# Attention loops of a four-layer GNN: SyncE awaits the ring's place before it loads row numbers, and a gather waits for the row numbers only

## The chip, the cores and the metric

The kernel runs on 1 core of one Trainium2 chip. Its time is the device time of one execution in microseconds (us). Before the change it is 5852.53 us, the median of 3 runs (5847.59 to 5857.74).

## The reference

Four graph layers follow each other on x (3125 nodes x 256 features, 100000 edges sorted by their target node), each behind a layer norm and a ReLU, each added to x. What matters here are layers 1 and 2, which hold the three attention loops:

```python
def _gatv2(x, src, dst, eattr, Wl, Wr, We, att, b, n):      # layer 1, twice
    xl = x @ Wl; xr = x @ Wr; ee = eattr @ We
    xj = xl[src]
    h = leaky_relu(xj + xr[dst] + ee, 0.2)
    logits = h @ att
    ex = exp(logits - segment_max(logits, dst, n)[dst])
    alpha = ex / segment_sum(ex, dst, n)[dst]
    return segment_sum(xj * alpha[:, None], dst, n) + b

# layer 2: four heads of 64
h = (x @ W).reshape(-1, 4, 64)
e = leaky_relu(einsum(h, att_src)[src] + einsum(h, att_dst)[dst], 0.2)
alpha = softmax of e over the edges of one dst
out = sigmoid(segment_sum(alpha[:, :, None] * h[src], dst).reshape(-1, 256) + bias)
```

Layer 0 is a weighted sum over neighbours, layer 3 a graph convolution; both are done by dense matrices of node pairs and are not touched.

## The kernel before

The edges are cut into 220 groups (NG) of 512 edges (4 tiles, T, of 128), all of a group with targets in one block of 128 nodes. A node stage writes a table of one row of 264 floats per node to DRAM. Then an attention loop goes over the groups: `edges1` and `edges2` (`gatv2_loop`, layer 1, once for each of its two convolutions), and `gat_edges` (`gat_loop`, layer 2).

The five engines run their own written-out programs and meet through semaphores. Each engine works in steps; in step s it handles group s minus the lag of the piece at hand, so that several groups are in flight. In `gatv2_loop`:

- GpSimd (POOL) gathers: for group t four indirect DMAs (L909), one per tile, take 128 table rows each by the row numbers in `m.src_col[t % 10]` and put them in the place `m.gath[t % 10]` of a ring of RG = 10 places (five are the buffer called gath, five lie in h, so a trace shows both names).
- SyncE (SP) loads: `load_list` brings the row numbers of group t from `g_src` into `src_col` (L889, 2 KB); `load` brings lin (L894, 2 KB), locrow (L895, one row laid out over 128 partitions, 128 KB) and eaT (L896, 12 KB) into rings of R = 5 places. SP is a queue in order: an instruction that waits holds all loads behind it.
- ScalarE (ACT) turns locrow into a 0/1 matrix of who is whose target (`place`, L1007 and L1010, lag 0), and copies and exponentials.
- TensorE (PE): `mix` (L1049, L1052, lag 1), `show_logits` (lag 3), `flip` (lag 4) and `sum_group` (L1071, lag 4), the last reader of the gathered rows, which raises `group_sum`.
- VectorE (DVE): `sum_inputs` (L921, lag 2) is the first reader of the gathered rows and waits for them; then `dot` (L928), `see` (L934), `add_linear` (L939, which raises `logits`), `add_group` (L980, lag 5), and small casts.

In `gat_loop` the same loads and gathers are L1111, L1117 and L1129. DVE does `place` (L1144, lag 0), reads the gathered rows first at L1157 (lag 1), weighs them at L1202 (lag 3), and does many pieces of 16 or 4 columns, some of them casts to bf16 (L1170, L1178, L1224, L1240); PE's last reader is `sum_group` (L1367, lag 4).

Before the change the place of group t in the ring of gathered rows is awaited by POOL: its first gather waits for `listed` (the row numbers have landed) and for `group_sum` of group t-10 (the place is free). In between it raises a semaphore `begun` that nobody waits for. SP loads the row numbers of group t once `logits` of group t-10 is there, and the three inputs of group t-5 directly behind it, on the same condition.

Of the kernel before, what the change touches and what calls it, by code (L numbers as in the profile page):

```python
# [32 lines left out]
R = 5  # L33
RG = 10
# [51 lines left out]
def drow(t, g):  # L86

    return t[bass.ds(g, 1), :].rearrange("a n -> (a n)")
# [28 lines left out]
def straight(stages, blocks=None, total=NG, unroll=U):  # L117

    deepest = max(lag for lag, _ in stages)
    of = [None] * total  # L120
    for s in range(total + deepest):
        if blocks and s % unroll == 0 and s < total:
            of[s:s + unroll] = blocks(s, unroll, s // unroll)
        for lag, stage in stages:
            t = s - lag
            if 0 <= t < total:
                stage(t, t % unroll, t // unroll, of[t])
# [12 lines left out]
def after(eng, sem, t, back=0, each=1):  # L140

    if not isinstance(t, int) or t >= back:
        eng.wait_ge(sem, (t - back + 1) * each)


def nth(u, turn, ring, unroll=U):

    return turn * (unroll // ring) + (u // ring + 1)
# [710 lines left out]
def gatv2_loop(nc, m, name, table, c):  # L859
# [6 lines left out]
    K = 3 * T  # L866
    with stage_of(nc, name) as (st, block):
        arrived, listed = st.sems("arrived", R), st.sems("listed", RG)
        gathered, begun = st.sems("gathered", RG), st.sem("begun")
        distance = st.sem("distance")  # L870
        placed, masked, mixed, summed = (st.sem(k) for k in ("placed", "masked", "mixed", "summed"))
        dotted, logits, hi_made, rest_made = (st.sem(k) for k in ("dotted", "logits", "hi_made", "rest_made"))
# [3 lines left out]
        weights, group_sum, done = (st.sem(k) for k in ("weights", "group_sum", "done"))  # L876
# [5 lines left out]
        @block.sync  # L882
        def _(sp):
            def by_column(src, t):
                return drow(src, t).rearrange("(p j) -> p j", j=T)

            def load_list(t, u, turn, b):
                after(sp, logits, t, RG)
                sp.dma_start(m.src_col[u % RG][:, :], by_column(m.g_src, t)).then_inc(listed[u % RG], 16)  # L889

            def load(t, u, turn, b):
                r = u % R
                after(sp, logits, t, R)
                sp.dma_start(m.lin[r][:, :], by_column(m.g_lin[c], t)).then_inc(arrived[r], 16)  # L894
                sp.dma_start(m.locrow[r][:, :], drow(m.g_locb, t).partition_broadcast(P)).then_inc(arrived[r], 16)  # L895
                sp.dma_start(m.eaT[r][0:KE, :], m.g_eaT[bass.ds(t, 1), :, :].rearrange("a k n -> (a k) n")  # L896
                             ).then_inc(arrived[r], 16)

            straight([(0, load_list), (RG - R, load)])

        @block.gpsimd
        def _(pool):
            def gather(t, u, turn, b):
                r = u % RG
                pool.wait_ge(listed[r], 16 * nth(u, turn, RG))
                after(pool, group_sum, t, RG)
                pool.sem_inc(begun, 1)
                for j in range(T):
                    pool.indirect_dma_start(m.gath[r][:, j, :], None, table,  # L909
                                            bass.IndirectOffsetOnAxis(m.src_col[r][:, j:j + 1], 0)  # L910
                                            ).then_inc(gathered[r], 16)

            straight([(0, gather)])
# [165 lines left out]
def gat_loop(nc, m, name, table):  # L1079
# [7 lines left out]
    WA = H * (DH + 1)  # L1087
    with stage_of(nc, name) as (st, block):
        arrived, listed = st.sems("arrived", R), st.sems("listed", RG)
        gathered, begun = st.sems("gathered", RG), st.sem("begun")  # L1090
        placed, masked, mixed, summed = (st.sem(k) for k in ("placed", "masked", "mixed", "summed"))
        pairs, logits, hi_made, rest_made = (st.sem(k) for k in ("pairs", "logits", "hi_made", "rest_made"))
        mid_made, parts, turned, copied = (st.sem(k) for k in ("mid_made", "parts", "turned", "copied"))
# [5 lines left out]
        group_sum, rescaled, done = (st.sem(k) for k in ("group_sum", "rescaled", "done"))  # L1099
# [7 lines left out]
        @block.sync  # L1107
        def _(sp):
            def load_list(t, u, turn, b):
                after(sp, logits, t, RG)  # L1110
                sp.dma_start(m.src_col[u % RG][:, :], drow(m.g_src, t).rearrange("(p j) -> p j", j=T)  # L1111
                             ).then_inc(listed[u % RG], 16)

            def load(t, u, turn, b):
                r = u % R
                after(sp, logits, t, R)
                sp.dma_start(m.locrow[r][:, :], drow(m.g_locb, t).partition_broadcast(P)).then_inc(arrived[r], 16)  # L1117

            straight([(0, load_list), (RG - R, load)])

        @block.gpsimd
        def _(pool):
            def gather(t, u, turn, b):
                r = u % RG
                pool.wait_ge(listed[r], 16 * nth(u, turn, RG))
                after(pool, group_sum, t, RG)
                pool.sem_inc(begun, 1)
                for j in range(T):
                    pool.indirect_dma_start(m.gath[r][:, j, :], None, table,  # L1129
                                            bass.IndirectOffsetOnAxis(m.src_col[r][:, j:j + 1], 0)  # L1130
                                            ).then_inc(gathered[r], 16)

            straight([(0, gather)])
# [669 lines left out]
def build(nc, a, out):  # L1803
    m = Memory()
    with ExitStack() as ctx:
# [82 lines left out]
        for c in (1, 2):  # L1888
            gatv2_nodes(nc, m, a, f"gatv2_{c}", c, tables[c - 1])
            gatv2_loop(nc, m, f"edges{c}", tables[c - 1], c)  # L1890
            batch_norm(nc, m, f"bn{c}", c, residual=(c == 2))
        layer_norm(nc, m, "ln2")
        gat_nodes(nc, m, a, "gat", tables[2])
        gat_loop(nc, m, "gat_edges", tables[2])
        gat_out(nc, m, "gat_out")
        layer_norm(nc, m, "ln3", scale=m.dinv)
# [37 lines left out]
```

## Time and profile before

| | |
|---|---|
| median of 3 runs | 5852.53 us |
| profiled execution, its own time | 5865.7 us |
| span of that execution in the trace | 5863.4 us |
| mean granted TensorE clock | 0.954 of full speed |
| PE busy | 4774.3 us, 81% |
| DVE busy | 4688.4 us, 80% |
| POOL busy | 3357.2 us, 57% |
| ACT busy | 3334.6 us, 57% |

Busy shares are means over the whole program; stages differ. The three attention loops take about 1131, 1131 and 1250 us of the span. A row of a timeline names the start, the duration, the engine, the line, and the tiles written and read; in brackets stands how long the engine sat idle before, and what ended it. "issue" means that the engine waited for nothing that the trace shows. Rows of SPq are the times at which SyncE issues a DMA, not the transfer. Ends of matmuls are modelled.

### The profile page before, as it was taken

Reading aid. Unit: us, or ns where it says so; the run is one execution under the profiler, and the core shown is the slowest. Engines: PE = TensorE matmul, PEld = TensorE weight load, DVE = VectorE, ACT = ScalarE, POOL = GpSimd, SP = SyncE. Lnnn points to the kernel's source line nnn. Section 1 sums busy time; section 2 is a strip of 40 time slices with the busy share of each in tenths; the row PEclk is TensorE's granted clock in tenths of the full one; section 3 lists DMA queues with packets and bytes.
Section 4 is the critical chain, followed back from the end, with each engine's and each line's share of the span. In section 5 each row is a group of like instructions: output and inputs, shape, how many; then the busy total and the mean of one; then the engine's idle time right before and its main releaser. Section 6 shows DMA issues by size and latency. Waiting matters only on the chain. (4 is left out here: it accounts for less than half of the span.)

```text
span 5863.4 us, 117927 instructions
## 1 busy us (share of the span) xinstructions
PE 4774.3 (81%) x30318; PEld 3499.0 (60%) x30319; DVE 4688.4 (80%) x18137; ACT 3334.6 (57%) x8375; POOL 3357.2 (57%) x3590
## 2 busy tenths in 40 slices
PE   0699888789779999998589999998377777777599
PEld 0344544568567777776277777776255555555388
DVE  4899999830588889888789888888699999999701
ACT  0677676610366667665466666666366666666500
POOL 1344444346477777776477777776177777777100
PEclk9899999889899999999899999999699999999899
DMA  4112233368255555554055555553154444444253
GB/s 91 33 57 81 88 97 100 100 234 308 100 128 135 134 134 135 134 135 107 31 138 134 134 134 135 134 134 90 48 131 123 120 120 119 120 120 121 68 148 110
DMA packets 591145, 695.30 MB, mean 119 GB/s; under 512 B 227684, under 2 KB 497297, under 8 KB 584443
## 3 DMA queue, kind: packets, MB, share of 16 engines
q0 software_dynamic: 128832, 362.75, 24.3%
q1 hardware_dynamic: 462010, 329.68, 20.7%
q14 instruction: 256, 2.09, 0.1%
q8 instruction: 47, 0.77, 0.1%
HBM read 589.91 MB, written 102.19 MB: 118 GB/s over the span
## 5 line engine op out<-in xcount | busy, mean ns | idle before, releaser
L909 POOL DMA_INDIRECT gath<-table,src_col x880 | 862.8, 980 | 277.0 <-issue 267.5
L909 POOL DMA_INDIRECT h<-table,src_col x880 | 861.6, 979 | 268.4 <-issue 268.4
L1049 PE MATMUL psum<-xr,ohT 128*128 x5280 | 812.4, 277 | 35.3 <-ACT ohT L1010 35.3
L742 DVE SCALAR_TENSOR_TENSOR xr<-xr,gath,psum 128x259 f32<-128x259 f32 x1440 | 682.7, 474 | 75.0 <-PE psum L728 63.9
L928 DVE SCALAR_TENSOR_TENSOR zs<-zs,mean 128x256 f32<-128x256 f32 x1760 | 645.3, 422 | 0.0
L1129 POOL DMA_INDIRECT gath<-table,src_col x440 | 440.0, 1000 | 285.8 <-issue 157.4
L728 PE MATMUL psum<-zs,locrow 128*128 128x259 f32 x1440 | 447.7, 450 | 164.9 <-DMA pairs<-xr 96.1
L1049 PEld LDWEIGHTS psum<-xr,ohT 128*128 128x128 bf16 x5280 | 505.8, 99 | 95.1 <-issue 36.9
L1208 DVE TENSOR_REDUCE seen<-psum 128x2 f32<-128x1024 f32 x440 | 518.2, 1219 | 39.1 <-PE psum L1348 21.4
L1129 POOL DMA_INDIRECT h<-table,src_col x440 | 437.2, 994 | 185.9 <-issue 185.9
L737 DVE TENSOR_SCALAR locrow<-psum,acc 128x128 f32<-128x128 f32 x1440 | 493.4, 343 | 7.3 <-POOL xr L678 7.3
L1071 PE MATMUL psum<-gath,prob 128*128 128x257 f32 x1760 | 432.4, 389 | 76.7 <-DVE acc L980 75.9
L694 ACT ACTIVATE xr<-irow,gath 128x128 f32<-128x128 f32 x1440 | 460.1, 390 | 51.1 <-PEq L172 0.7
L1052 PE MATMUL psum<-We,eaT 128*128 128x256 bf16 x1760 | 486.6, 276 | 0.0
L1071 PE MATMUL psum<-h,prob 128*128 128x257 f32 x1760 | 432.4, 389 | 58.8 <-DVE acc L980 57.2
L728 PEld LDWEIGHTS psum<-zs,locrow 128*128 128x128 f32 x1440 | 281.7, 216 | 329.7 <-issue 151.4
L997 ACT CAST rows<-psum 128x128 bf16<-128x128 f32 x440 | 117.1, 266 | 582.0 <-PE psum L1033 582.0
L771 PE MATMUL psum<-h,xr 128*128 128x256 f32 x1900 | 418.9, 383 | 5.6 <-DMA xr<-pairs 5.6
L1071 PEld LDWEIGHTS psum<-gath,prob 128*128 128x128 f32 x1760 | 316.3, 189 | 159.2 <-issue 122.0
L771 PEld LDWEIGHTS psum<-h,xr 128*128 128x128 f32 x1900 | 365.1, 192 | 58.3 <-DMA xr<-pairs 7.4
L1071 PEld LDWEIGHTS psum<-h,prob 128*128 128x128 f32 x1760 | 319.1, 191 | 128.0 <-issue 67.2
L921 DVE TENSOR_TENSOR zs<-psum,h 128x1024 f32<-128x1024 f32 x220 | 269.4, 1224 | 151.3 <-DMA h<-table,src_col 91.9
(314 smaller groups left out, 11618.3 us busy)
## 6 DMA issues: line engine op xcount, KB each, us to landing
locrow<-g_locb SPq DMA_DIRECT2D x660, 128.0 KB
pairs<-xr SPq DMA_DIRECT2D x640, 128.9 KB
xr<-pairs SPq DMA_DIRECT2D x13, 1716.0 KB
gath<-table,src_col POOLq DMA_INDIRECT x1320
h<-table,src_col POOLq DMA_INDIRECT x1320
xr<-pairs SPq DMA_DIRECT2D x25, 832.0 KB
acc<-pairs SPq DMA_DIRECT2D x12, 1716.0 KB
xr<-pairs SPq DMA_DIRECT2D x13, 1584.0 KB
```

Source lines behind the costliest of these rows:

```text
L694: ins = nc.scalar.activation(gap[u % 2][:, j, :], m.irow[:, :], ACT.Abs, bias=col(t["low"], t4 * 4 + j))
L728: nc.tensor.matmul(m.ps[j][:, 0:EXTRA + 3], pick[(u * 4 + j) % 8], rhs[u % 4][:, j, :], start=True, stop=True).then_inc(product, 1)
L737: nc.vector.tensor_scalar(pick[u % 8], numbers, t["key"][:, g:g + 1], None, ALU.is_equal).then_inc(keyed, 1)
L742: nc.vector.scalar_tensor_tensor(kept[:, u, 0:EXTRA + 3], kept[:, (u - 1) % HELD, 0:EXTRA + 3], t["same"][:, g:g + 1], m.ps[u % 4][:, 0:EX ...
L771: mm = nc.tensor.matmul(sums_of(m, hb), lhs(i, hb), m.h[:, db, :], start=False, stop=(db == NB - 1 and (hb % 2 == 1 or hb == n - 1)))
L909: pool.indirect_dma_start(m.gath[r][:, j, :], None, table, bass.IndirectOffsetOnAxis(m.src_col[r][:, j:j + 1], 0)).then_inc(gathered[r], 16)
L928: ins = nc.vector.scalar_tensor_tensor(m.zs[q][:, j, :], m.zs[q][:, j, :], 0.0, m.att_relu[:, :], ALU.max, ALU.mult, accum_out=m.dots[:, j ...
L1049: nc.tensor.matmul(zb[q][:, j, :], m.ohT[r][:, e], blk(m.xr3, b, s * D, (s + 1) * D), start=(s == 0), stop=False)
L1052: mm = nc.tensor.matmul(zb[q][:, j, :], m.eaT[r][:, e], m.We12[c][:, :], start=False, stop=True)
L1071: mm = nc.tensor.matmul(sum_ps[:, 0:WA], m.prob[:, 0, j * P:(j + 1) * P], m.gath[u % RG][:, j, 0:WA], start=(j == 0), stop=(j == T - 1))
L1129: pool.indirect_dma_start(m.gath[r][:, j, :], None, table, bass.IndirectOffsetOnAxis(m.src_col[r][:, j:j + 1], 0)).then_inc(gathered[r], 16)
L1208: ins = nc.vector.tensor_reduce(m.seen[:, 2 * q:2 * q + 2], m.psum[:, 2 * q:2 * q + 2, :], AX.X, ALU.max)
```

## The change

In both loops four things change. SP's `load_list` waits for `group_sum` of group t-10 where it waited for `logits` of group t-10. `load` has a lag of 4 (RG - R - 1) where it had 5, so behind the list of group s come the inputs of group s-4. POOL's wait for `group_sum` is gone. The semaphore `begun` and its increment are gone.

```diff
@@ gatv2_loop
-        gathered, begun = st.sems("gathered", RG), st.sem("begun")
+        gathered = st.sems("gathered", RG)
...
             def load_list(t, u, turn, b):
-                after(sp, logits, t, RG)
+                after(sp, group_sum, t, RG)
                 sp.dma_start(m.src_col[u % RG][:, :], by_column(m.g_src, t)).then_inc(listed[u % RG], 16)
...
-            straight([(0, load_list), (RG - R, load)])
+            straight([(0, load_list), (RG - R - 1, load)])
...
                 pool.wait_ge(listed[r], 16 * nth(u, turn, RG))
-                after(pool, group_sum, t, RG)
-                pool.sem_inc(begun, 1)
                 for j in range(T):
...
@@ gat_loop
-        gathered, begun = st.sems("gathered", RG), st.sem("begun")
+        gathered = st.sems("gathered", RG)
...
-                after(sp, logits, t, RG)
+                after(sp, group_sum, t, RG)
                 sp.dma_start(m.src_col[u % RG][:, :], drow(m.g_src, t).rearrange("(p j) -> p j", j=T)
...
-            straight([(0, load_list), (RG - R, load)])
+            straight([(0, load_list), (RG - R - 1, load)])
...
                 pool.wait_ge(listed[r], 16 * nth(u, turn, RG))
-                after(pool, group_sum, t, RG)
-                pool.sem_inc(begun, 1)
```

On SyncE, in `edges1`, at the end of the loads that wait for nothing (src_col are row numbers, lin, locrow and eaT the inputs), the program before reads:

```order
L896 DMA eaT<-g_eaT 12x512
L889 DMA src_col<-g_src 128x4
L894 DMA lin<-g_lin 128x4
L895 DMA locrow<-g_locb 128x512
L896 DMA eaT<-g_eaT 12x512
L889 DMA src_col<-g_src 128x4 [waits edges1_logits]
L894 DMA lin<-g_lin 128x4 [waits edges1_logits]
L895 DMA locrow<-g_locb 128x512
```

and the changed one, at the same place:

```order
L896 DMA eaT<-g_eaT 12x512
L889 DMA src_col<-g_src 128x4
L894 DMA lin<-g_lin 128x4 [waits edges1_logits]
L895 DMA locrow<-g_locb 128x512
L896 DMA eaT<-g_eaT 12x512
L889 DMA src_col<-g_src 128x4 [waits edges1_group_sum]
L894 DMA lin<-g_lin 128x4 [waits edges1_logits]
L895 DMA locrow<-g_locb 128x512
```

The inputs stand one list earlier in the queue, and from the eleventh list on the whole queue is held by `group_sum`, which comes later than `logits` of the same group. The very first inputs stand behind 5 lists where there were 6.

On GpSimd, in `edges1`, where the ring comes round for the first time (the names of the semaphores of `listed` are those of earlier stages that had the same number), the program before reads:

```order
L909 DMA h<-table,src_col 128x264 [waits steps_gathered2]
L909 DMA h<-table,src_col 128x264 x3
L909 DMA gath<-table,src_col 128x264 [waits const_stacked,edges1_group_sum]
L909 DMA gath<-table,src_col 128x264 x3
L909 DMA gath<-table,src_col 128x264 [waits list_done,edges1_group_sum]
L909 DMA gath<-table,src_col 128x264 x3
```

and the changed one (its L907 is L909 of before):

```order
L907 DMA h<-table,src_col 128x264 [waits steps_gathered2]
L907 DMA h<-table,src_col 128x264 x3
L907 DMA gath<-table,src_col 128x264 [waits const_stacked]
L907 DMA gath<-table,src_col 128x264 x3
L907 DMA gath<-table,src_col 128x264 [waits list_done]
L907 DMA gath<-table,src_col 128x264 x3
```

The gathers stand in the same order; the wait for `group_sum` is gone from the first of each four.

## Rows read from the trace of the kernel before

**Rows 1.** The page's first part: busy us of each engine, share of the span, instructions.

```profile
PE 4774.3 (81%) x30318; PEld 3499.0 (60%) x30319; DVE 4688.4 (80%) x18137; ACT 3334.6 (57%) x8375; POOL 3357.2 (57%) x3590
```

**Rows 2.** Windows of the three loops: length, busy PE, PEld, DVE, ACT, POOL; clock, DMA.

```profile
1627.00:2758.00 1131.00, 1035.32 (x7424) 826.37 (x7424) 1002.83 (x4366) 775.78 (x1530) 862.09 (x880) 0.99 0.57 134
2932.00:4058.00 1126.00, 1036.13 (x7427) 827.32 (x7428) 1002.69 (x4373) 775.00 (x1530) 857.87 (x876) 0.99 0.56 134
4227.00:5477.00 1250.00, 967.26 (x8922) 680.13 (x8923) 1198.03 (x5014) 799.68 (x2820) 877.15 (x880) 0.98 0.47 119
```

**Rows 3.** Lines L907 and L1127, GpSimd's wait on the ring: ns min/median/max.

```profile
L907 POOLq EVENT_SEMAPHORE  x440: 17/43/43, 1626.8 to 4036.2; - x147
...
L1127 POOLq EVENT_SEMAPHORE  x220: 17/3642/6086, 4226.4 to 5437.9; - x110
```

**Rows 4.** Timeline of GpSimd in edges1: start, us, line, tiles, idle.

```profile
2539.09 0.95 POOL L909 DMA_INDIRECT h<-table,src_col  x1 [0.31 <-issue]
2540.34 1.06 POOL L909 DMA_INDIRECT h<-table,src_col  x1 [0.30 <-issue]
2541.70 0.95 POOL L909 DMA_INDIRECT h<-table,src_col  x1 [0.30 <-issue]
```

**Rows 5.** Timeline of the same step of edges1, other engines.

```profile
2536.51 0.33 SPq L889 DMA_DIRECT2D src_col<-g_src  x1
...
2537.02 1.97 PE L1071 MATMUL psum<-gath,prob 128*128 128x257 f32 x8 [0.39 <-DVE acc L980]
...
2538.20 1.23 DVE L921 TENSOR_TENSOR zs<-psum,h 128x1024 f32<-128x1024 f32 x1 [0.47 <-DMA h<-table,src_col]
...
2540.01 0.72 ACT L1007 ACTIVATE locrow<-locrow,minus_icol 128x512 bf16<-128x512 bf16 x1
```

**Rows 6.** Timeline, start of edges1.

```profile
1625.16 2.71 SPq L889 DMA_DIRECT2D src_col<-g_src  x6
1628.86 0.40 SPq L896 DMA_DIRECT2D eaT<-g_eaT  x1
...
1627.59 1.02 POOL L909 DMA_INDIRECT gath<-table,src_col  x1 [4.59 <-DMA src_col<-g_src]
...
1631.81 0.72 ACT L1007 ACTIVATE locrow<-locrow,minus_icol 128x512 bf16<-128x512 bf16 x1 [10.00 <-DMA eaT<-g_eaT]
```

**Rows 7.** Timeline, end of edges1, when SyncE loads nothing more.

```profile
2741.28 1.14 POOL L909 DMA_INDIRECT h<-table,src_col  x1 [0.30 <-issue]
...
2744.37 1.22 DVE L921 TENSOR_TENSOR zs<-psum,h 128x1024 f32<-128x1024 f32 x1 [0.49 <-DMA h<-table,src_col]
```

**Rows 8.** Timeline of one step of gat_edges.

```profile
4810.25 1.99 PE L1367 MATMUL psum<-h,prob 128*128 128x260 f32 x8
...
4812.56 0.17 DVE L1224 CAST new<-new 128x4 bf16<-128x4 f32 x1
...
4813.02 0.94 POOL L1129 DMA_INDIRECT h<-table,src_col  x1 [0.56 <-issue]
...
4813.40 0.18 DVE L1178 CAST parts<-rest 128x16 bf16<-128x16 f32 x1
...
4813.71 0.37 DVE L1144 TENSOR_SCALAR ohT<-locrow,icol 128x512 bf16<-128x512 bf16 x1
```

**Rows 9.** Timeline of another step of gat_edges.

```profile
4619.41 0.94 POOL L1129 DMA_INDIRECT gath<-table,src_col  x1 [0.56 <-issue]
...
4620.02 0.34 DVE L1178 CAST parts<-rest 128x16 bf16<-128x16 f32 x1
```

**Rows 10.** Timeline, line L1144, steps 11 and 19, then 53 and 59.

```profile
4297.16 0.35 DVE L1144 TENSOR_SCALAR ohT<-locrow,icol 128x512 bf16<-128x512 bf16 x1
...
4342.41 0.34 DVE L1144 TENSOR_SCALAR ohT<-locrow,icol 128x512 bf16<-128x512 bf16 x1
...
4536.81 0.37 DVE L1144 TENSOR_SCALAR ohT<-locrow,icol 128x512 bf16<-128x512 bf16 x1
...
4570.10 0.37 DVE L1144 TENSOR_SCALAR ohT<-locrow,icol 128x512 bf16<-128x512 bf16 x1
```

## The prediction

> **What bounds the kernel now.** I read the page first, for what each engine does over the whole span. DVE is busy 80% and POOL 57% [rows 1], so POOL does not look like a limit. Then the windows of the three loops, which together are 3507 of the 5863.4 us. In the two gatv2 loops POOL is busy 862 of 1131 us, that is 76%, behind PE (92%) and DVE (89%); in gat_edges DVE has 1198 of 1250 us, 96% [rows 2]. The share misleads in the gatv2 loops: the timeline of POOL shows gathers of 0.95 us with 0.30 us between any two, and "issue" beside each gap, so nothing else is waited for [rows 4]. Four gathers and four gaps are 4 x (0.95 + 0.30) = 5.0 us. One of the four is 0.11 us longer in the step shown, and 1131 / 220 = 5.14 us is what a group takes. So POOL issues without a break from the first to the last group; DVE's first reader L921 sits idle 0.47 us until the gather's data is there [rows 5].
>
> Next I looked at the wait that the change removes. On POOL the wait for group_sum lasts at most 43 ns over all 440 groups of the gatv2 loops: the place in the ring is always free there. In gat_edges it lasts 3.6 us in the median: there the ring is full, POOL is ahead, and DVE sets the pace [rows 3].
>
> **POOL's instructions.** A wait and an increment less per group. The gap in front of a group's first gather (0.30 or 0.31 us) is like the other three [rows 4], so the two short instructions are hidden in the time that an issue takes anyway. Bounds: nothing, or at most the 43 ns of the wait [rows 3] on each of 440 groups, 19 us faster. I take 0, by the equal gaps. In gat_edges POOL is not the limit: 0 either way.
>
> **The row numbers are asked for later.** SP issues the list of group t after group_sum of t-10. From issue to the first gather that waits for it the loop's start shows 1627.59 - 1625.16 = 2.43 us [rows 6]. In the gatv2 loops: the PE row is group_sum of t-3, t being the group whose L921 stands in the same rows; it ends at 2538.99, 0.79 us after L921 [rows 5]. Group_sum of t-9, which frees the place of t+1, ended six groups of 5.13 us earlier, at 2508.2, and the first gather of t+1 is two gathers and their gaps before that at 2539.09, at 2536.6 [rows 4]. So there are 28 us for 2.43: nothing is late. In gat_edges the ring is full, and here the latency does go in front of each gather: group_sum ends at 4810.25 + 1.99 = 4812.24 and the gather starts 0.78 us later [rows 8]; it becomes some 2.5 us, 1.7 us later. Its data is read first by L1157 of step t+1, while group_sum of t-10 was step t-6: seven steps of 5.55 us less 5.5 us for the gathers leaves 33 us. Nothing is late here either.
>
> The Trainium skill ("DMA: Bandwidth & Descriptors", Anatomy of one DMA) gives about 2.0 us as the fixed part of any DMA, whatever its size, which speaks against putting a second DMA in series in front of each gather. The 2.43 us measured agree. By that rule alone, with the ring full in the gatv2 loops too, 440 groups would be 2 us later each.
>
> **The inputs are asked for later.** Every load behind the list is held too. On SP behind group_sum of t-3 stand the list of t+7 and lin, locrow and eaT of t+3. The queue gets free at 2538.99; one list issue is 0.33 us [rows 5], the others 0.40 to 0.43, as eaT at the start [rows 6], with 0.04 between them, so eaT is issued at about 2540.36. eaT and what stands before it landed 1631.81 - 1628.86 = 2.95 us after eaT's issue [rows 6]: 2543.3. ACT's L1007 in the rows is the place of t+2 [rows 5]; that of t+3 comes one group later, at 2545.14. Slack 1.8 us in a normal step; over all steps of edges1 the distance from the end of group_sum to that L1007 is 5.52 us at least, so 1.2 us at the tightest. Before, SP issued at 2536.51, triggered by logits [rows 5], 2.5 us sooner. Cost 0, as long as the landing under load stays under 4.1 us. In gat_edges the same distance is 11.6 us at least: no risk.
>
> **Loop starts.** One list less, 2.71 / 6 = 0.45 us, in front of the first inputs [rows 6]. In the gatv2 loops POOL's chain of gathers starts with the first list and is the limit: 0. In gat_edges DVE gains 0.45 us.
>
> **What the moved DMAs meet.** Two small couplings remain, and they are of the size that can be measured. First, in the gatv2 loops: gathers that start 2.0 to 2.2 us after L921's start, among DVE's L928, are longer. There are 154 of them in edges1 and 149 in edges2, with a mean of 0.16 us on top of 0.95: 24 + 24 = 48 us on the limiting engine. The row at 2540.34 is one (2.14 us after 2538.20, 1.06 us long) [rows 4, 5]. Their place is set by the landing time of the gather before, and the excess falls by 0.02 us for each 0.02 us that the gather starts later against L921. At the loop's end, with no loads in flight, landing takes 2744.37 - 2742.42 = 1.95 us [rows 7], against about 2.0 with them. So moving the loads can take off up to 0.05 x 303 = 15 us, or add the like, if they now meet the last gather of a group. I take 0.
>
> Second, in gat_edges DVE itself is slowed when a cast to bf16 starts 0.55 to 0.7 us after a gather's start: L1178 takes 0.34 instead of 0.18 us [rows 8, 9]. With POOL waiting on the ring the gathers keep one phase, and steps 53 to 59 take 33.29 / 6 = 5.55 us; before the ring is full the phase drifts and steps 11 to 19 take 45.25 / 8 = 5.66 us [rows 10]. So a phase at random costs 0.10 us a step more than the phase of now. The change moves the phase by 1.7 us, for the 175 groups from the 45th on. The first gather then starts some 1.0 to 1.2 us after L1144, the third and fourth 3.5 and 4.8 us after it. L1224 and L1178 start 1.15 and 0.31 us before the next L1144 [rows 8], that is at 4.4 and 5.24 us in a step of 5.55, so they would start 0.9 and 0.4 us after a gather: just free of both, with 0.15 us to spare. I take 0; bounds -8 us (what is left of such meetings now) and +0.38 x 175 = 66 us.
>
> The Trainium skill ("SBUF — State Buffer", Who interferes with whom) says that VectorE and GpSimd share a pair of ports as an exclusive lock, and that reductions never take part. The longer casts agree. The rule gives no price for this phase.
>
> **Sum.** 0 (POOL) + 0 (lists) + 0 (inputs) - 0.45 (start of gat_edges) + 0 (couplings) = -0.45 us on the profiled execution, 5865.7 us. That one is 13 us above the median of the runs, 5852.5, so I forecast 5852.
>
> **Rivals.**
>
> *A. The new phase in gat_edges meets the casts (slower).* Place: L1224, L1178 or L1244 on DVE. For it: my margin of 0.15 us is no larger than what I don't know of SP's wake-up and of the landing under load. Against it: the free band is as wide as the bands that cost. Price: 0.10 to 0.20 us a step x 175 = 18 to 35 us, 5870 to 5888. It decides when the list lands 0.1 to 0.3 us sooner or later than 2.43 us.
>
> *B. The gathers' excess in the gatv2 loops shrinks (faster).* Either landing is 0.05 us faster (15 us), or it becomes over 0.08 us slower, and the fourth gather then starts before the window and loses its whole excess: up to 48 us. 5805 to 5838. Against it: nothing that fixes the phase (POOL's landing, DVE's order) is edited.
>
> *C. The wait on POOL was not hidden (faster).* 19 us at most, 5833. Against it: the equal gaps.
>
> *D. The inputs land late in the gatv2 loops (slower).* If locrow, 128 KB, needs 6 us beside gathers that keep the DMA engines 57% busy [rows 2], ACT is late by 0.5 to 1 us in each group, after 0.5 us that POOL's pace leaves: some 0.3 x 440 = 130 us, 5980. Against it: it would need twice the 2.95 us of the start.
>
> *E. The full ring of gat_edges, but in the gatv2 loops as well:* 1.7 x 440 = 750 us slower. Excluded nearly by the 43 ns.
>
> **Chances.** Forecast 0.44, A 0.26, B 0.17, C 0.07, D 0.05, E 0.01. A measurement of this kernel can tell about 0.2% (12 us) from no change. Faster by more than that 0.24, within 0.44, slower 0.32. The likeliest case's own range is 5841 to 5864. The range over all takes in A and most of B: 5820 to 5892.
>
> **What would show it.** Right: POOL's gaps in the gatv2 loops stay 0.30 us, both loops stay near 1131 us, L1007 shows no wait for a DMA, and in gat_edges the first gather starts about 2.5 us after group_sum's end with steps at 5.55 us. Wrong by A: steps in gat_edges of 5.65 us or more with casts over 0.25 us. By B: the fourth gather of a group near 0.95 us. By C: gaps under 0.30 us at every fourth gather. By D: idle time of ACT in front of L1007, ended by a DMA.

## The result and the profile after

The changed kernel takes 5859.39 us (median of 20 runs, 5851.90 to 5867.82), the kernel before 5849.84 us in the same series (20 runs, 5844.17 to 5858.32). The ratio of the runs is 1.0015 with an interval of 1.0008 to 1.0022: 9.5 us slower. That is 7 us above the forecast of 5852 and inside the range of 5820 to 5892. But the interval lies wholly above 1: the kernel became slower by a small, measurable amount, where the forecast had half a microsecond.

The profiled execution after has a span of 5858.9 us, before 5863.4 us. This pair stands the other way round, since the profiled execution of before, 5865.7 us, lies 16 us above the median of its runs. Differences are therefore read loop by loop and not from the whole span. A loop is counted here from its first load of row numbers to the end of its last gather (gatv2), or to its last L1144 (gat_edges), in us:

| | edges1 | edges2 | gat_edges | the rest |
|---|---|---|---|---|
| before | 1132.6 | 1132.8 | 1251.8 | 2346.3 |
| after | 1125.4 | 1124.4 | 1263.2 | 2345.9 |

Two opposite changes, of 7 to 8 us in each gatv2 loop and of 11 us in gat_edges, stand behind a small sum. The windows of the three loops say the same, with POOL's busy time in the gatv2 loops down from 862.09 and 857.87, and DVE's in gat_edges up from 1198.03 [rows 2]. The view is that of the windows of the kernel after: length, then busy us (and instructions) of PE, PEld, DVE, ACT, POOL, then clock, DMA.

```profile
1618.00:2744.00 1126.00, 1029.04 (x7424) 825.34 (x7424) 994.07 (x4366) 771.31 (x1530) 855.75 (x880) 0.99 0.55 135
2910.00:4035.00 1125.00, 1026.40 (x7424) 824.42 (x7424) 993.99 (x4366) 771.42 (x1530) 854.47 (x880) 0.99 0.55 135
4204.00:5468.00 1264.00, 964.40 (x8923) 677.74 (x8923) 1206.20 (x5014) 800.02 (x2822) 847.10 (x880) 0.98 0.47 118
```

**The gatv2 loops.** Lines stand two to four lower after the change: L907 is L909 of before, L919 is L921, L926 is L928, L1005 is L1007. The timeline of the kernel after, edges1, shows one group of gathers end and its first reader start:

```profile
2521.20 0.95 POOL L907 DMA_INDIRECT h<-table,src_col  x1 [0.30 <-issue]
2521.83 0.33 SPq L889 DMA_DIRECT2D src_col<-g_src  x1
2522.45 0.95 POOL L907 DMA_INDIRECT h<-table,src_col  x1 [0.30 <-issue]
2522.69 0.43 SPq L895 DMA_DIRECT2D locrow<-g_locb  x1
2523.70 0.95 POOL L907 DMA_INDIRECT h<-table,src_col  x1 [0.30 <-issue]
2526.20 0.95 POOL L907 DMA_INDIRECT h<-table,src_col  x1 [0.30 <-issue]
2526.64 1.23 DVE L919 TENSOR_TENSOR zs<-psum,h 128x1024 f32<-128x1024 f32 x1 [0.53 <-DMA h<-table,src_col]
2528.70 1.13 POOL L907 DMA_INDIRECT h<-table,src_col  x1 [0.30 <-issue]
```

The gather at 2522.45 is the last of its group (counted back from the change of buffer names). It ends at 2523.40, and L919, which waits for nothing but this data, starts 3.24 us later. Before, the last gather of the group started at 2535.20, ended at 2536.27, and L921 started at 2538.20 [rows 5], 1.93 us later:

```profile
2535.20 1.07 POOL L909 DMA_INDIRECT h<-table,src_col  x1 [0.30 <-issue]
```

Over all groups whose first reader sat idle until the gather's data was there, the median of this landing is 1.99 us before (132 in edges1, 134 in edges2) and 3.06 and 3.04 us after (107 and 104; four fifths of them from 2.6 to 3.8). What travels beside the last gather is new: locrow (128 KB) is issued at 2522.69, during the gather, with lin (2 KB) just before and eaT (12 KB) just behind it; before, SyncE issued its loads from 2536.51 on [rows 5], when the last gather had ended.

The late landing shifts VectorE's steps against the gathers. The fourth gather of a group started 2.06 us (median) behind the L921 before it; it now starts 1.18 us behind L919. In both traces gathers of edges1 that start up to 1.2 us behind that instruction take 0.95 us, and those that start 2.0 to 2.2 us behind it 1.11 (means). By place in the group the mean gather of edges1 was 0.957, 0.951, 0.948 and 1.063 us; it is 1.004, 0.954, 0.947 and 0.984. The fourth loses most of its excess, the first takes some up (the row at 2528.70 is a first one, 2.06 us after L919). The sum falls from 3.919 to 3.890 us, 0.029 x 220 = 6 us in the loop, and the gaps stay 0.305 us on the mean at each of the four places. The chain from the first gather's start to the last one's end went from 1130.21 and 1130.40 to 1123.54 and 1122.40 us.

**gat_edges.** Here L1125 is L1129 of before, L1174 is L1178, L1220 is L1224, L1240 is L1244, L1140 is L1144 and L1363 is L1367. The timeline of the kernel after:

```profile
4842.35 0.35 DVE L1140 TENSOR_SCALAR ohT<-locrow,icol 128x512 bf16<-128x512 bf16 x1
4843.23 0.94 POOL L1125 DMA_INDIRECT h<-table,src_col  x1 [2.66 <-DMA src_col<-g_src]
4844.42 1.99 PE L1363 MATMUL psum<-h,prob 128*128 128x260 f32 x8
4846.74 0.17 DVE L1220 CAST new<-new 128x4 bf16<-128x4 f32 x1
4846.98 0.95 POOL L1125 DMA_INDIRECT h<-table,src_col  x1 [0.30 <-issue]
4847.59 0.34 DVE L1174 CAST parts<-rest 128x16 bf16<-128x16 f32 x1
4847.68 0.25 DVE L1240 TENSOR_TENSOR new<-new_rest,new 128x4 bf16<-128x4 f32 x1
4848.06 0.35 DVE L1140 TENSOR_SCALAR ohT<-locrow,icol 128x512 bf16<-128x512 bf16 x1
4848.94 0.94 POOL L1125 DMA_INDIRECT h<-table,src_col  x1 [1.02 <-DMA src_col<-g_src]
```

The gather now waits for its row numbers and starts 0.88 us after L1140; group_sum ended at 4844.42 + 1.99 = 4846.41, 2.53 us before the gather at 4848.94, and these 2.5 us were forecast. The fourth gather starts at 4846.98, and the cast L1174 stands 0.61 us behind it and takes 0.34 us where it took 0.18 [rows 8]. L1240, which stands behind it in VectorE's order, is long too (0.25 us). Both end at 4847.93, and there the gather ends. The step is 5.71 us where it was 5.55. Over the loop the median step went from 5.550 to 5.710 us; of 219 steps 159 were under 5.6 us and now 69 are, while those of 5.6 to 6.1 us went from 45 to 136.

The gather's end sets how long the cast is held. In five traces (before, after, e4, f1, f4; the runs come below) 453 of these casts (L1178 of before) started over 0.45 us before the end of the gather beside them: none took more than 0.21 us, though the gather was running. Another 370 started 0.43 to 0.18 us before its end: all 370 ended within 0.02 us behind the gather's end and took up to 0.43 us.

### The profile page after: what moved, and what is told of

Read it like the earlier page. It is cut to its first block and busy times, and to the rows that moved or that the text cites. A ratio compares the mean times of both kernels' runs of the same rounds, so it can differ in the third digit from the quotient of the medians.

```text
span 5858.9 us, 117267 instructions
## 1 busy us (share of the span) xinstructions
PE 4758.4 (81%) x30318; PEld 3493.5 (60%) x30319; DVE 4679.6 (80%) x18137; ACT 3325.8 (57%) x8375; POOL 3312.2 (57%) x3590
## 5 line engine op out<-in xcount | busy, mean ns | idle before, releaser
L907 POOL DMA_INDIRECT gath<-table,src_col x880 | 855.5, 972 | 275.8 <-issue 267.6
L907 POOL DMA_INDIRECT h<-table,src_col x880 | 854.7, 971 | 268.2 <-issue 268.2
L926 DVE SCALAR_TENSOR_TENSOR zs<-zs,mean 128x256 f32<-128x256 f32 x1760 | 646.1, 422 | 0.0
L1125 POOL DMA_INDIRECT gath<-table,src_col x440 | 423.2, 962 | 314.5 <-DMA src_col<-g_src 201.8
L1125 POOL DMA_INDIRECT h<-table,src_col x440 | 423.9, 963 | 199.9 <-issue 112.4
L919 DVE TENSOR_TENSOR zs<-psum,h 128x1024 f32<-128x1024 f32 x220 | 269.3, 1224 | 150.2 <-DMA h<-table,src_col 90.4
```

Source lines behind the costliest of these rows:

```text
L907: pool.indirect_dma_start(m.gath[r][:, j, :], None, table, bass.IndirectOffsetOnAxis(m.src_col[r][:, j:j + 1], 0)).then_inc(gathered[r], 16)
L926: ins = nc.vector.scalar_tensor_tensor(m.zs[q][:, j, :], m.zs[q][:, j, :], 0.0, m.att_relu[:, :], ALU.max, ALU.mult, accum_out=m.dots[:, j ...
L1125: pool.indirect_dma_start(m.gath[r][:, j, :], None, table, bass.IndirectOffsetOnAxis(m.src_col[r][:, j:j + 1], 0)).then_inc(gathered[r], 16)
```

## The experiments

Each was timed against the kernel before on the same chip. There are five sets on five chips: the e runs up to e4, e5 to e8, the f runs, the g runs and the h runs. **Theory 1**, from the profile: in gat_edges the moved phase puts a gather in front of the casts and costs some 11 us; in the gatv2 loops the later inputs delay the landing, move VectorE against the gathers and give 7 to 8 us in each loop. **Rivals**: that the time in gat_edges goes with the later list itself and not with the phase; that the gain comes from the wait and the increment which POOL no longer has; that it comes from the list.

### Which loop loses and which gains

**e1_gat_only** is the kernel before with the change in `gat_loop` only; **e2_gatv2_only** has it in `gatv2_loop` only.

> The change in gat_edges alone; both gatv2 loops as before. Theory 1 (in gat_edges the gathers now start 0.9 us after L1144 instead of 0.7 us before the next one, and casts of VectorE meet them): about 11 us slower than before, median step of L1144 5.71 us, gatv2 loops as before. Rival (the slowdown comes from the gatv2 loops, where a gather's landing went from 2.0 to 3.0 us): no difference from before, within 4 us.

> The change in the two gatv2 loops alone; gat_edges as before. Theory 1: 0 to 15 us faster than before, as in the profile after the chain of gathers is 7 to 8 us shorter in each loop (fewer gathers held up by VectorE). Rival (the gatv2 loops are where the change loses): some 9 us slower. Median step of gat_edges 5.55 us either way.

e1: 5861.04 against 5858.65 us, ratio 1.0005 (0.9996 to 1.0014). Its gat_edges took 1252.2 us with a median step of 5.56 us (125 steps under 5.6 us, 79 of 5.6 to 6.1), its gatv2 loops 1129.7 and 1131.2. e2: 5845.49, ratio 0.9978 (0.9969 to 0.9987); gatv2 loops 1124.0 and 1125.2 with a landing of 3.1 us, gat_edges 1247.0 with 5.55 us a step. So the gain in the gatv2 loops is shown, 13 us together; the loss in gat_edges points the right way but its interval takes in no change.

How far single traces scatter is seen from the later ones, on chips where the kernel before takes some 5850 us. By the measure of the table above, gatv2 loops as in the kernel before took 1129.7 to 1133.2 us (before, e1, e4, f4), and changed ones 1123.1 to 1125.4 (after, e2, e3, f1). A gat_edges as in the kernel before took 1247.0 to 1250.4 us in e2, f2, f3, h1 and h2, and 1251.8 in the first trace.

### Phase or list

**e3_wait_raised** is the changed kernel with one wait more on POOL in front of a group's first gather in gat_edges, so that the gather starts elsewhere in DVE's step while the row numbers stay late:

```diff
                 pool.wait_ge(listed[r], 16 * nth(u, turn, RG))
+                after(pool, raised, t, 7)
```

> The changed kernel, and in gat_edges the first gather of group t also waits for raised of group t-7, a small piece of VectorE at 4.3 us of a step. That moves its start from 0.9 to about 5.0 us after L1144, the pause between the fourth and the next first gather then lies over the casts. Theory 1: steps of 5.55 us, gat_edges 11 us shorter than in the changed kernel, and the whole 0 to 15 us faster than before. Rival (the list's latency or the moved loads slow gat_edges, whatever the phase): steps stay at 5.71 us, the whole as the changed kernel or slower by the added wait.

5843.79 us, ratio 0.9979 (0.9970 to 0.9988). The first gather starts 5.0 us after DVE's `place` (133 of 160 groups, from the 61st on), the median step is 5.58 us with 165 under 5.6 us, and gat_edges takes 1248.4 us. With the late list kept and the phase moved away the loss is gone, though the gathers start 4 us later still than in the changed kernel: that they are late is not what costs.

**e4_phase_alone** is the kernel before, list and all, with a wait that is to give the phase of the changed kernel; **e8_phase_earlier** is the same with an earlier event of DVE, **f4_phase_earlier** that kernel once more:

```diff
                 after(pool, group_sum, t, RG)
+                after(pool, parts, t, 7)        # e4
+                after(pool, top_parts, t, 8)    # e8, f4
```

> The kernel before; in gat_edges the first gather of group t also waits for parts of group t-7 (L1182, which ends 0.1 us after L1144 starts). Its start moves from 0.7 us before to about 0.85 us after L1144; lists and loads stay where they were. Theory 1: steps of about 5.7 us and some 12 us (0.2%) slower than before, from the phase alone. Rival (list latency or moved loads): steps of 5.55 us and no difference.

> The kernel before; in gat_edges the first gather also waits for top_parts of group t-8, which ends some 0.15 us ahead of parts, the event of the run before. Theory 1 refined (a step costs 0.1 to 0.2 us more when a gather starts 4.55 to 4.70 us after L1144, and nothing at 4.75): first gather at 0.85 us, fourth at 4.6 us after L1144, steps of 5.65 to 5.71 us, gat_edges 15 to 25 us longer than with parts (1246.7 us). Rival (the phase is no cause): steps of 5.52 to 5.55 us as there.

> The kernel before, gat_edges' first gather also waits for top_parts of t-8. Where the kernel before takes 5850 us, theory 1 refined: first gather 0.85 us after L1144, fourth at 4.6, steps of 5.65 to 5.71 us, gat_edges 15 to 25 us longer than the 1246.7 us with parts. Rival: steps of 5.52 to 5.55 us as there. Where it takes 6795 us: no reading of the phase, within 0.3% of before.

e4: 5852.17 us, ratio 0.9991 (0.9982 to 1.0000). This is the number of the rival and not mine. But the phase came out 0.1 us later than I had built it for: the first gather starts 1.0 us after `place` (144 of 160 groups) where the changed kernel has 0.9 in its slow steps. The timeline of e4:

```profile
4834.44 0.97 POOL L1130 DMA_INDIRECT gath<-table,src_col  x1 [0.30 <-issue]
4834.92 0.18 DVE L1179 CAST parts<-rest 128x16 bf16<-128x16 f32 x1
4835.23 0.35 DVE L1145 TENSOR_SCALAR ohT<-locrow,icol 128x512 bf16<-128x512 bf16 x1
4836.20 0.95 POOL L1130 DMA_INDIRECT gath<-table,src_col  x1 [0.80 <-issue]
```

and that of f4:

```profile
4832.96 0.94 POOL L1130 DMA_INDIRECT gath<-table,src_col  x1 [0.30 <-issue]
4833.57 0.34 DVE L1179 CAST parts<-rest 128x16 bf16<-128x16 f32 x1
4833.66 0.25 DVE L1245 TENSOR_TENSOR new<-new_rest,new 128x4 bf16<-128x4 f32 x1
4834.04 0.35 DVE L1145 TENSOR_SCALAR ohT<-locrow,icol 128x512 bf16<-128x512 bf16 x1
4834.82 0.99 POOL L1130 DMA_INDIRECT gath<-table,src_col  x1 [0.92 <-DVE new L1245]
```

In e4 the cast stands 0.48 us behind a gather's start and takes 0.18 us; in f4 it stands 0.61 us behind and takes 0.34. f4: 5871.80 us, ratio 1.0023 (1.0013 to 1.0033), gat_edges 1260.5 us with a median step of 5.70; e4 had 1246.7 and 5.52. Neither has the changed list, both have the same gatv2 loops as before (f4: 1131.2 and 1130.7 us). A shift of POOL's gathers by 0.2 us within VectorE's step (the first one 0.97 us behind `place` in the rows of e4, 0.78 in those of f4) is worth 14 us. This pair shows that the phase alone costs; together with e3 it rules out the list. e8 ran on a chip on which everything is longer (below): 6776.23 us, ratio 0.9971 (0.9960 to 0.9983); it is not read for the phase.

### The sum, on other chips

**e5_changed_again**, **f1_changed_again** and **g1_changed_third** are the changed kernel again, on three chips.

> The changed kernel itself, timed beside the others on one chip. Its two halves alone gave +0.05% (gat_edges) and -0.22% (gatv2 loops) on one chip. Theory 1 (the halves add up, and gat_edges costs 0 to 12 us depending on where the fourth gather falls): between -0.2% and +0.05%, both gatv2 chains near 1123 us, gat_edges 1252 to 1263 us. Rival (the halves work on each other): +0.15% again with gatv2 chains longer than 1125 us.

> The changed kernel once more. In the last set the kernel before took 6795 us (engines stand still for up to 44 us at a time there) and the change cost 4.9%, since GpSimd waited 937 us for lists in the gatv2 loops. If the chip of this set is one where the kernel before takes some 5850 us: theory 1 (halves add up) -0.2% to +0.05%, gatv2 chains near 1123 us; rival +0.15% as first measured. If it is like the last one: +5% again.

> The changed kernel on one more chip. Theory (gatv2 loops 7 to 8 us shorter each, gat_edges 2 to 15 us longer by how many of its steps have a gather at 4.55 to 4.70 us): between -0.25% and +0.05%; rival (the first measurement was the rule): +0.15%. On a chip whose engines stand still at times: up to +5%.

f1: 5849.54 against 5857.74 us, ratio 0.9984 (0.9975 to 0.9993), faster. Its gatv2 loops took 1124.7 and 1124.0 us, as in the first series; its gat_edges 1256.5 with as many steps below 5.6 as between 5.6 and 6.1 us (102 each), against 69 and 136 in the first. The same gat_edges thus falls into the casts more or less often. Of 220 casts L1178 (by its line of before) those over 0.25 us were 38 in the kernel before, 57 in e1, 74 in f1 and 113 in the kernel after. What makes the difference between these three is not shown. With 13 us of gain on one side and 2 to 11 us of loss on the other (e1's runs, the traces of the first series), and the first series slower where f1 is faster, the sum has no fixed sign.

On the chips of e5 and g1 the kernel before takes 6794.54 and 6800.13 us instead of 5850, and the change costs 5%: 7137.51 us, ratio 1.0489 (1.0463 to 1.0516), and 7120.03, ratio 1.0477 (1.0462 to 1.0493). What stands still there are waits that the trace puts down to "remote", up to 44 us at once, in loops of the kernel before as well (43.5 us in e8). Of the waits of g1, the changed kernel: us in total, times, longest.

```profile
POOL gath L907 <- DMA src_col<-g_src: 447.0, 135, 16.3
DVE zs L919 <- remote: 446.2, 145, 35.4
POOL h L907 <- DMA src_col<-g_src: 427.3, 148, 8.6
```

In the gatv2 loops POOL waits 874 us for row numbers. The next two rows are GpSimd's wait on the ring, in ns (min, median, max): first in e8, whose gatv2 loops are those of before, on such a chip, then in f4, likewise, on one where the kernel takes 5858 us.

```profile
L907 POOLq EVENT_SEMAPHORE  x440: 17/4587/29770, 1621.2 to 4671.9; - x147
```

```profile
L907 POOLq EVENT_SEMAPHORE  x440: 17/43/43, 1627.9 to 4032.4; - x147
```

On such a chip the ring is full in the gatv2 loops too, and then the list stands in series in front of each gather: the mechanism of rival E. But the gatv2 loops are only half of the cost. In g1 the three loops took 1512, 1515 and 1693 us; on the same chip the gatv2 loops of g3 (described below), whose list is at its old time, took 1438 and 1440, and gat_edges as before took 1533 in g3 and 1534 in g2. So some 75 us are lost in each gatv2 loop and 160 in gat_edges, where the ring is full on the chips of 5850 us too [rows 3] and the prediction put the cost of the later list at nothing. What holds the engines up there, and why a ring of ten places doesn't hide a list of 2.5 us, is open.

### What in the gatv2 loops gives the gain

**e6_loads_first** and **f2_loads_first** have gat_edges as before; in the gatv2 loops the list waits for group_sum and POOL for the list alone, as in the change, but the inputs stand ahead of the list:

```diff
-            straight([(0, load_list), (RG - R, load)])
+            straight([(RG - R, load), (0, load_list)])
```

**e7_loads_later_alone** and **f3_loads_later_alone** have the gatv2 loops of before, POOL's wait and increment kept, and move SyncE's inputs:

```diff
                 after(sp, logits, t, R)
+                after(sp, group_sum, t, 6)
...
-            straight([(0, load_list), (RG - R, load)])
+            straight([(0, load_list), (RG - R - 1, load)])
```

> Only the gatv2 loops differ from the kernel before: GpSimd waits for the list alone and the list for group_sum, as in the change, but SyncE issues the inputs of group s-5 ahead of the list of group s, on logits, at the old time. Theory 2 (the inputs, asked for later, travel beside the last gather of a group; its data lands 1 us later, VectorE's phase against the gathers breaks up, and fewer gathers are held up): landing stays near 2.0 us, GpSimd's chain near 1130 us, no gain over before. Rival (the wait taken from GpSimd, or the later list, brings it): chains near 1123 us and 0.2% faster.

> Only SyncE's inputs in the gatv2 loops are moved, behind group_sum of t-6, with the lag of 4; the list's wait for logits and GpSimd's wait for group_sum stay as before. Theory 2: landing near 3.1 us, chains near 1123 us, 0.2% faster than before. Rival: landing 2.0 us, chains 1130 us, no difference.

> Gatv2 loops only: GpSimd awaits the list alone, the list awaits group_sum, the inputs are issued ahead of it at their old time. Where the kernel before takes 5850 us, theory 2 (the later inputs lengthen the landing and break VectorE's phase): landing 2.0 us, chains 1130 us, no gain. Rival: chains 1123 us, 0.2% faster. Where it takes 6795 us: +2.9% again.

> Gatv2 loops only: the inputs are moved behind group_sum of t-6, list and GpSimd's waits as before. Where the kernel before takes 5850 us, theory 2: landing near 3.1 us, chains near 1123 us, 0.2% faster. Rival: 2.0 us, 1130 us, no difference. Where it takes 6795 us: +0.4% again.

f2: 5843.89 us, ratio 0.9977 (0.9968 to 0.9987); loops 1124.5 and 1124.2, landing 3.1 us. f3: 5846.20 us, ratio 0.9976 (0.9967 to 0.9985); loops 1123.6 and 1122.8, landing 3.2 us. f3 has the whole gain with POOL's wait and increment in place, and the gap in front of a gather is 0.305 us on the mean in both: one rival is out. f2 doesn't tell the list from the inputs, by a flaw of mine: SyncE's queue is in order, and a list that waits for group_sum holds the inputs behind it anyway. On the chip where the kernel before takes 6794.54 us, e6 took 6990.93, ratio 1.0290 (1.0276 to 1.0303), e7 6825.13, ratio 1.0038 (1.0021 to 1.0055).

The next pair parts them. **g2_list_late_alone** and **h1_list_late_again** put the list two groups behind and the inputs ahead of it, so that only the list waits for group_sum and the inputs go with logits; **g3_inputs_late_alone** and **h2_inputs_late_again** leave the list on logits and hold the inputs alone; POOL's wait is kept in these two:

```diff
# g2, h1: list on group_sum, POOL waits for the list alone
+            straight([(RG - R, load), (2, load_list)])
# g3, h2: list on logits
+                after(sp, group_sum, t, 6)      # in load
+            straight([(0, load_list), (6, load)])
```

> Gatv2 loops only. SyncE issues the inputs of group s-5 on logits, at their old time, and behind them the list of group s-2 on group_sum of s-12; GpSimd waits for the list alone. So the list alone is late. If the small row-number load beside the last gather makes it land late: landing 3.1 us, chains 1123 us, 0.2% faster. If the 128 KB of locrow do: 2.0 us and 1130 us, no gain.

> Gatv2 loops only. SyncE issues the list of group s on logits, at its old time, and behind it the inputs of group s-6 on group_sum of s-12; GpSimd waits as before. So the inputs alone are late. If the 128 KB of locrow beside the last gather make it land late: landing 3.1 us, chains 1123 us, 0.2% faster. If the list does: 2.0 us and 1130 us.

> Gatv2 loops only: inputs at their old time, the list alone on group_sum, GpSimd waits for the list alone. Where the kernel before takes 5850 us: landing 3.1 us and chains of 1123 us if the small row-number load is what makes the last gather land late; 2.0 us and 1130 us if the inputs do. Where it takes 6800 us: +1.7% again, from the list's latency.

> Gatv2 loops only: the list at its old time, the inputs alone on group_sum, GpSimd waits as before. Where the kernel before takes 5850 us: landing 3.1 us and chains of 1123 us if the inputs (128 KB of locrow) make the last gather land late; 2.0 us and 1130 us if the list does. Where it takes 6800 us: +0.2% again.

h1: 5850.40 against 5852.22 us, ratio 0.9998 (0.9989 to 1.0007), landing 1.97 us. h2: 5844.15, ratio 0.9982 (0.9973 to 0.9991), landing 3.1 and 3.2 us, chains of gathers 1122.70 and 1122.05 us (h1: 1127.54 and 1125.49). The timeline of h2:

```profile
2502.79 1.06 POOL L910 DMA_INDIRECT gath<-table,src_col  x1 [0.30 <-issue]
2503.13 0.43 SPq L896 DMA_DIRECT2D locrow<-g_locb  x1
2504.15 0.95 POOL L910 DMA_INDIRECT gath<-table,src_col  x1 [0.30 <-issue]
2506.96 1.22 DVE L922 TENSOR_TENSOR zs<-psum,gath 128x1024 f32<-128x1024 f32 x1 [1.05 <-DMA gath<-table,src_col]
```

and that of h1:

```profile
2521.12 0.43 SPq L895 DMA_DIRECT2D locrow<-g_locb  x1
2523.89 1.10 POOL L907 DMA_INDIRECT h<-table,src_col  x1 [0.31 <-issue]
2525.59 0.43 SPq L895 DMA_DIRECT2D locrow<-g_locb  x1
2526.90 1.23 DVE L919 TENSOR_TENSOR zs<-psum,h 128x1024 f32<-128x1024 f32 x1 [0.45 <-DMA h<-table,src_col]
```

In h2 locrow is issued during the last gather, which ends at 2503.85, and the reader starts 3.11 us later. In h1 the locrows are issued 2.8 us before the last gather's start and 0.6 us after its end, and the reader starts 1.91 us after that end. So the inputs alone are enough for the late landing and the whole gain. The late list alone doesn't bring the late landing: it is issued 1.3 us before the last gather's start (median of edges1) in h1, against 0.1 us before it in the changed kernel, and the landing stays 1.97 us. Its chains are 1127.54 and 1125.49 us, where gatv2 loops as before have 1127.2 to 1130.8 (before, e1, e4, f4); a gain of some 2 us from the later list or the missing wait is not excluded. Which of the three inputs does it was not parted, since lin, locrow and eaT move together. On a chip where the kernel before takes 6800.13 us, g2 took 6920.98, ratio 1.0173 (1.0158 to 1.0188), and g3 6814.05, ratio 1.0019 (1.0007 to 1.0030): there, in the gatv2 loops, the late list is the part that costs.

### The better versions

**g4_both_gains** has the changed gatv2 loops and e4's gat_edges.

> The change in the gatv2 loops, and in gat_edges the kernel before with the first gather also waiting for parts of group t-7 (first gather 1.0 us after L1144, fourth at 4.75). The two alone gave -0.22% and -0.09%. Theory: -0.2% to -0.35%, chains 1123 us, gat_edges 1247 us. Rival: as the gatv2 half alone.

It ran on the chip of 6800.13 us and took 6962.33, ratio 1.0240 (1.0217 to 1.0264); the late list is in it. How it does where the kernel takes 5850 us wasn't measured. Of what was, e2, e3, f2, f3 and h2 are the fastest there, 0.18 to 0.24% faster than the kernel before. h2, the inputs later alone, is the one I would take: 0.18% faster there, and (as g3) 0.19% slower where the whole change costs 5%.

## Why the prediction was right or wrong

**POOL's instructions: 0, right.** The gaps stay 0.30 us, also in front of a group's first gather, and f3, which keeps both instructions, takes 5846.20 us where f2, which has neither, takes 5843.89, within their intervals. Rival C is refuted.

**Row numbers later, inputs later: 0, right as far as the data goes.** ACT's L1005 sat idle for a DMA 4 times in 440, 20.1 us in all, as L1007 did in e1, whose gatv2 loops are those of before (4 times, 21.2 us). Rival D is refuted. The estimate of SyncE's timing held as well: the list comes 2.53 us before the gather, where 2.5 were forecast. This holds for the chips of 5850 us; on the others the later list costs. What the prediction takes from the Trainium skill ("DMA: Bandwidth & Descriptors", Anatomy of one DMA), 2.0 us, describes a DMA that GpSimd issues, and the list is issued by SyncE; its 2.43 and 2.53 us are this case's own figures.

**The first coupling, taken as 0: wrong, by 13 us.** The step that failed is the sentence against rival B that nothing fixing the phase of the gatv2 loops is edited. I had used the moved issue time of the inputs to ask whether they come late, and measured the landing of a gather only at the loop's end with nothing beside it (1.95 us [rows 7]) and with the loads where they were. Both were about 2.0, and from that I took the loads to be without effect on it. They are, as long as the inputs are not issued beside the last gather; there the landing is 3.1 us. Rival B had the mechanism (a landing over 0.08 us slower, the fourth gather free of its excess) and overrated its size: of 48 us for the two loops 13 (e2's runs) to 16 (the windows by loop above) came, since the first gather of a group takes up part of what the fourth loses, and the landing scatters (four fifths from 2.6 to 3.8 us), so that gathers of every place now fall into the long stretch at times.

**The second coupling, taken as 0: wrong, by 2 to 11 us.** That is rival A, at its place and by its sign: steps of 5.71 us and casts of 0.34. The place was off by less than 0.2 us: I put the fourth gather 4.8 us behind `place`, it stands 4846.98 - 4842.35 = 4.63 us behind it. The step that failed is the margin of 0.15 us, which took two moving things as fixed.

The first is the latency. From the 61st group on 124 of 160 first gathers waited for their row numbers. They started 2.56 us after the list's issue in the median, which is near the forecast, but four fifths of them lie from 2.34 to 2.79 (in f1 from 2.12 to 2.85), wider than the margin on either side. The second is the step. A cast that is held moves `place` of the next step later, while the gather follows group_sum: group_sum ended 4813.71 - 4812.24 = 1.47 us before `place` [rows 8], in a slow step 4848.06 - 4846.41 = 1.65.

Both lead to the same place. In the kernel after, slow steps (5.6 to 6.1 us) behind a step under 5.6 us had the first gather 2.39 us behind group_sum and 0.91 behind `place` (medians), those behind a slow step 2.54 and 0.89. And slow steps come about as often either way, so they do not hold each other up. From the 61st step on, 63 of 102 steps behind a slow one were slow in the kernel after and 31 of 48 behind one under 5.6 us; in f1 35 of 74 and 33 of 76. In the kernel before it was 1 of 23 and 18 of 127. In the kernel after the cast stands 0.61 us behind the gather in the slow steps (median) and 0.52 in a fast one after a slow one. The bound of 66 us used 0.38 us a step, for which the prediction shows no row.

The Trainium skill ("SBUF — State Buffer", Who interferes with whom) has VectorE and GpSimd share ports under an exclusive lock. It has the one that comes second blocked for the whole instruction. The casts agree in part. The 370 held ones ended with the gather, as by a lock that it gives back; but 453 others took at most 0.21 us while the gather was running, so in these traces the block is not there for the whole 0.95 us. That the price hangs on 0.1 us of phase is the trace's alone.

**The sum: near by luck.** The forecast of 5852 had no term but 0.45 us; the measured time has one of 13 us and one of the other sign that nearly cancel: the sum is +9.5 us in the first series, -8.2 in f1, and -10.8 by adding e1 and e2. In the first pair of traces the loops add to -15.6 + 11.4 = -4.2 us, with a profiled execution of before 16 us above its median. The other 14 us lie between this pair and the medians. Some 5 of them are in the three loops of the first trace, which are long beside the same loops in later traces (2 x 1.3 us in the gatv2 loops, 2.9 in gat_edges, against the means of the traces named above); the rest stays open, as a trace of an execution near the median of before is not there.

**What was not in the range:** the 5% of e5 and g1. Rival E had the mechanism and 1% of the chances, on the evidence of a ring wait of 43 ns [rows 3], which holds for the chips of 5850 us and not for all. Half of the 5% comes from gat_edges, where the row numbers asked for later were put at 0 and no rival had them.

## What to carry to other kernels

An engine whose starts are tied to another's by a wait has a phase, and a change of who waits for what moves it: list the short instructions that stand within some tenths of a microsecond of the partner's starts, with their durations at both phases, and treat a margin below the scatter of the latency that sets the phase as none. Look at the ends too: here an instruction was held until its partner's end, so the price is the rest of the partner's time. Moving a load is not free because its data is still in time: look at what it now travels beside. And a buffer that is deep enough in one trace is not deep enough everywhere: a latency put in series behind a ring's wait cost nothing of its own on one kind of chip, even where the ring was full (e3), and was the main part of 5% on the other.

## What the runs showed of the hardware

Loads of 2, 128 and 12 KB issued together beside an indirect gather of 128 rows made the gather's data usable 3.1 instead of 2.0 us after the gather's end (h2 against h1). A cast of 128 x 16 to bf16 took 0.34 instead of 0.18 us when it started 0.61 us after a gather, and 0.18 at 0.48 us (f4, e4). In five traces all 370 casts that started 0.43 to 0.18 us before a gather's end ended with it, and none of the 453 that started over 0.45 us before it took more than 0.21 us. From the issue of a 2 KB list to the start of the gather that waited for it 2.56 us passed (median of 124 in gat_edges of the kernel after), in four fifths of the cases 2.34 to 2.79. Of the five chips of the experiments the kernel before took 5852 to 5859 us on three and 6795 to 6800 on two, with waits of up to 44 us there for which the trace names no engine of the core.
